# MoE with MLP and KAN experts: at least one pair of MLP blocks ahead of the first KAN layer in place of two, and ScalarE's weight copies ahead of its notes of rows

## What is computed

```python
x = x + 0.5 * moe(layernorm(x), ...)
x = x + attention_block(layernorm(x), ...)      # window of 128, 16 heads, gated FFN
x = x + 0.5 * moe(layernorm(x), ...)

# moe: 8 experts, top 2; 4 are MLPs and 4 are KANs
w_full = top-2 softmax weights of x @ gate_W     # per token
h = gelu(x @ mlp_W1 + mlp_b1)                    # 128 -> 512
mlp_out = h @ mlp_W2 + mlp_b2                    # 512 -> 128
h0 = layernorm(x, kan_ln_g0, kan_ln_b0)
basis0 = 1 - tanh((h0 - grid) / 2) ** 2          # 8 grid points: 128 -> 1024
z = basis0 @ kan_sl_W0 + kan_sl_b0               # 1024 -> 256
h1 = layernorm(z, kan_ln_g1, kan_ln_b1)
basis1 = 1 - tanh((h1 - grid) / 2) ** 2          # 256 -> 2048
kan_out = basis1 @ kan_sl_W1 + kan_sl_b1         # 2048 -> 128
out = sum of the experts' outputs by w_full
```

## Time and profile before

| | us |
|---|---|
| median of three runs | 637.17 |
| lowest and highest | 632.69, 643.67 |
| the profiled execution, whole | 639.1 |
| its span, first to last instruction | 637.3 |
| PE, DVE, ACT, POOL busy in it | 558.2, 454.3, 401.1, 262.1 |

### The profile page before, as it was taken

How to read it: one execution, slowest core, us unless ns; L and a number is a source line. 1 busy time by engine, 2 the same in 40 slices (tenths; PEclk the granted TensorE clock), 3 DMA queues, 4 the chain that set the end, 5 groups by cost and what they waited for, 6 DMA issues and landing times. The chain is left out here.

```text
span 637.3 us, 19397 instructions
## 1 busy us (share of the span) xinstructions
PE 558.2 (88%) x6514; PEld 494.5 (78%) x6515; DVE 454.3 (71%) x1135; ACT 401.1 (63%) x954; POOL 262.1 (41%) x314
## 2 busy tenths in 40 slices
PE   9677899999999488888889888998788999999970
PEld 8666899999999355766778783688788999999970
DVE  6734768788788576699678788557466787878864
ACT  4645868889875158710456523256587789888943
POOL 7144556555544345820000013221455556656540
PEclk7768989999999869999999999985798999999995
DMA  8793222100101220000100039303111000110106
GB/s 264 246 407 100 67 62 86 45 26 29 33 16 19 68 78 3 4 3 14 16 5 4 5 120 402 156 29 114 34 30 26 25 27 27 33 29 25 29 18 202
DMA packets 41433, 46.58 MB, mean 73 GB/s; under 512 B 7409, under 2 KB 33377, under 8 KB 40353
## 3 DMA queue, kind: packets, MB, share of 16 engines
q1 hardware_dynamic: 32272, 33.99, 15.9%
q0 software_dynamic: 4736, 9.71, 5.5%
q10 hardware_dynamic: 4368, 2.10, 1.1%
HBM read 35.69 MB, written 10.09 MB: 72 GB/s over the span
## 5 line engine op out<-in xcount | busy, mean ns | idle before, releaser
L881 PE MATMUL k_y_ps<-kan_w,k_basis 128*128 x1056 | 128.5, 281 | 7.3 <-DVE k_basis L978 7.3
L881 PEld LDWEIGHTS k_y_ps<-kan_w,k_basis 128*128 128x128 f32 x1056 | 124.4, 196 | 9.6 <-issue 9.2
L871 PE MATMUL k_z_ps<-kan_w,k_basis 128*128 x528 | 120.5, 381 | 0.6 <-issue 0.6
L1151 ACT ACTIVATE k_sig<-k_h1T 128x256 f32<-128x256 f32 x264 | 84.4, 402 | 47.5 <-DVE k_h1T L1005 47.4
L871 PEld LDWEIGHTS k_z_ps<-kan_w,k_basis 128*128 128x128 f32 x528 | 98.2, 191 | 13.3 <-issue 1.1
L978 DVE SCALAR_TENSOR_TENSOR k_basis<-k_sig 128x512 f32<-128x512 f32 x132 | 88.1, 690 | 14.6 <-ACT k_sig L1151 14.6
L1817 ACT ACTIVATE got<-p_ps 128x960 f32<-128x960 f32 (+1 forms) x44 | 39.2, 944 | 42.0 <-PE p_ps L1672 41.9
L1144 ACT ACTIVATE k_sig<-k_h0T 128x128 f32<-128x128 f32 x280 | 59.2, 294 | 7.6 <-DVE k_h0T L966 7.6
L697 POOL DMA_INDIRECT y_rows<-k_y,k_rows x33 | 34.3, 1041 | 53.8 <-DVE j_y L1033 28.3
L849 PE MATMUL m_z_ps<-m_xT,m_w 128*128 128x128 f32 x304 | 43.3, 289 | 8.1 <-ACT m_w L1173 4.9
L849 PEld LDWEIGHTS m_z_ps<-m_xT,m_w 128*128 128x128 f32 x304 | 41.4, 202 | 11.1 <-ACT m_w L1173 6.3
(11 more groups left out here) (270 smaller groups left out, 1089.5 us busy)
## 6 DMA issues: line engine op xcount, KB each, us to landing
kan_w<-in_L_ffn_kan_sl_W_dram SPq DMA_DIRECT2D x16, 1024.0 KB, 14.0
x_rows<-got SPq DMA_DIRECT2D x16, 256.0 KB, 2.5
mlp_w<-in_L_ffn_mlp_W_dram SPq DMA_DIRECT2D x2, 1024.0 KB, 5.9
mlp_w<-in_L_ffn_mlp_W_dram SPq DMA_DIRECT2D x8, 256.0 KB, 6.7
got<-y_rows SPq DMA_DIRECT2D x8, 256.0 KB, 4.9
got<-y_rows ACTq DMA_DIRECT2D x8, 256.0 KB, 5.4
xs<-in_L_attn_x_dram SPq DMA_DIRECT2D x4, 256.0 KB, 3.8
s_cos<-in_cos_dram SPq DMA_DIRECT2D x8, 128.0 KB
```

What stands on the lines that cost most here:

```text
L871: last = nc.tensor.matmul(z_ps, basis0[:, g], k.kan_w0[:, bass.ds(e, 1), g], start=(g == 0), stop=(g == G - 1))
L881: last = nc.tensor.matmul(y_ps, basis1[:, g, c], k.kan_w1[:, bass.ds(e, 1), c, g], start=(g == 0 and c == 0), stop=(g == G - 1 and c == F2 ...
L1151: ins = nc.scalar.activation(sig1[:, g], h1T[:], ACT.Sigmoid, bias=float(-GRID[g]))
```

## The change

It has three parts.

- DVE, L405: the lower bound under the halving goes from 5.0 to 3.0, so that `pairs` is at least 1 in place of 2. The bound asserted in `counts` follows.
- POOL: no blocks ahead of the loop any more. A pass gathers and scatters block 2 ii + 1, then block 2 ii + 2, and then waits for both stores and frees both `m_y`. The two waits behind the loop are gone.
- ACT: its loop starts at 0 as well. Only the note for block 1 stands ahead of it. In a pass the copy of the weights for block 2 ii + 4 stands ahead of the note for block 2 ii + 2, and this note waits for `m_y_free` to be 2 ii + 2, where it waited for `m_stored[1]`.

```diff
@@ route, DVE
-                link(nc.vector.tensor_scalar(pairs_i[:], spread[:], 1.0, 5.0, ALU.add, ALU.max))
+                link(nc.vector.tensor_scalar(pairs_i[:], spread[:], 1.0, 3.0, ALU.add, ALU.max))
@@ counts
-            for v, low, high in zip(found, (2, 1, 1, 9), (MAXB // 2 + 1, MAXB, MAXB, MAXB)):
+            for v, low, high in zip(found, (1, 1, 1, 9), (MAXB // 2 + 1, MAXB, MAXB, MAXB)):
@@ moe_blocks, POOL
-                for u in range(2):
-                    m_gather(1 + u, u)
-                    m_scatter(1 + u, u)
-                with pool.Fori(1, pairs) as ii:
+                with pool.Fori(0, pairs) as ii:
                     for u in range(2):
-                        j = 2 * ii + (1 + u)
-                        pool.wait_ge(m_stored[u], ii * 16)
+                        m_gather(2 * ii + (1 + u), u)
+                        m_scatter(2 * ii + (1 + u), u)
+                    for u in range(2):
+                        pool.wait_ge(m_stored[u], ii * 16 + 16)
                         pool.sem_inc(m_y_free, 1)
-                        m_gather(j, u)
-                        m_scatter(j, u)
 
                 pool.wait_ge(turned, 2)
                 pool.sem_inc(noted, 1)
                 get_rows(x_in, rows_first[:, 2], loaded)
-                pool.wait_ge(m_stored[0], pairs * 16)
-                pool.sem_inc(m_y_free, 1)
                 power(0)
                 m_scatter(2 * pairs + 1, 0)
-                pool.wait_ge(m_stored[1], pairs * 16)
-                pool.sem_inc(m_y_free, 1)
@@ moe_blocks, ACT
-                _, *e_first = mlp_experts(act, 0, 5)
+                _, *e_first = mlp_experts(act, 0, 3)
                 m_take_w1(first, e_first[0])
                 note_rows(1, 0)
-                note_rows(2, 1)
                 sigmoids0(0)
                 m_take_w1(2, e_first[1])
                 act.preload_act_table(ACT.Gelu)
                 gelu(first)
-                m_take_w1(3, e_first[2])
-                gelu(2)
-                m_take_w1(4, e_first[3])
-                gelu(3)
-                act.wait_ge(m_stored[0], 16)
-                note_rows(3, 0)
-                with act.Fori(1, pairs) as ii:
+                with act.Fori(0, pairs) as ii:
                     _, *e_pair = mlp_experts(act, 2 * ii + 2, 3)
                     m_take_w1(2 * ii + 3, e_pair[0])
                     gelu(2 * ii + 2)
-                    act.wait_ge(m_stored[1], ii * 16)
+                    m_take_w1(2 * ii + 4, e_pair[1])
+                    act.wait_ge(m_y_free, 2 * ii + 2)
                     note_rows(2 * ii + 2, 1)
-                    m_take_w1(2 * ii + 4, e_pair[1])
                     gelu(2 * ii + 3)
                     act.wait_ge(m_stored[0], ii * 16 + 16)
                     note_rows(2 * ii + 3, 0)
```

## The result

| | before | after |
|---|---|---|
| median of 11 runs each, us | 633.86 | 640.70 |
| lowest and highest | 630.4, 643.67 | 637.32, 643.9 |
| ratio of the runs, with its 95% interval | | 1.009 [1.0061, 1.0119] |
| the profiled execution, whole | 639.1 | 641.56 |
| its span, first to last instruction | 637.3 | 639.7 |

The change makes the kernel slower by 0.9%: 5.7 us, by the interval 3.9 to 7.5. The ratio compares fast runs, and two runs of before, 643.67 and 643.64, count as slow; with them the means differ by 4.2 us. The forecast was 639.8 us, which is 2.6 above the 637.2 that the three runs shown gave. The two profiled executions differ by 2.5 us. So the forecast met the difference of the profiles, and the difference of the runs is about twice that.

The account below looks back on a forecast made before the run. The prediction took TensorE (PE) to bound both mixtures. First mixture -0.4 us, second +3.0, ACT's reordering and the jumps back zero: +2.6 on the 637.2 us median of three runs, so 639.8 us, range 633 to 645.

Parts of the forecast that it names:

- A: The forecast itself, both mixtures: -0.4 us in the first, +3.0 us in the second, 639.8 us; 50%.
- D: Loops on ACT and POOL: jumps back fetch code, 1.26 us in POOL's chain on top of A, 641.1 us; 14%.
- Block counts, joint rounds: First mixture: 1 pair, 13 joint rounds of 9.25 us and 2 alone of 7.71; the second mixture keeps 2 pairs.
- First KAN matmul: First mixture: weights land at 50.4 us, then 0.5 us of register reads, so 50.9 us (50.4 to 51.7).
- First KAN group: First mixture, L871: 3.62 us at full clock plus 1.7 for one fall of the clock, 5.3 us.
- Sum of the first mixture: First KAN product 3.5 us earlier, two more joint rounds cost 3.1 us: -0.4 us (-2.6 to +0.4).
- Second mixture: POOL's new order delays PE's first KAN group by 1.3 us, plus 1.7 for the clock: +3.0 us (0.1 to 4.1).
- The bound: First mixture, one pair less ahead of KAN and two more joint rounds: -0.4 us.
- C: First mixture: the clock doesn't fall behind the wait for KAN weights either, and B holds; 634.7 us; 12%.
- E: Joint rounds: POOL's slip is carried on, 3.6 us in each of 13 rounds, 684 us, slower by over 2%; 3%.
- B: Second mixture: POOL's wait is free, x_in lands in time, the clock stays up; -0.4 + 0.1, 636.9 us; 16%.

Follow-up runs that it names:

- the order alone: The kernel before with the new order on GpSimd and ScalarE but the old bound 5.0, two pairs in both mixtures; ratio to before 0.999 [0.9949, 1.0031].
- the bound alone: The kernel before with bound 3.0 in the first mixture only, GpSimd and ScalarE in the old order; ratio to before 1.0083 [1.0049, 1.0117].
- the kernel that kept PE busy: The kernel after, with 20 repetitions of small unread matmuls ahead of PE's wait for the KAN weights; ratio to before 1.007 [1.0026, 1.0113].

## Why the prediction came out right, and where its steps were off

**The total** (640.7 against 639.8) and its place within 2% hold, and the nearness is luck. Two errors cancel in it: the median of before was 633.86 over eleven runs, 3.3 us below the 637.2 of three from which I counted, and the change was +5.7 us, 3.1 more than my +2.6. Beneath it the steps read off single profiles came mostly as written, with three sizes off. But the two parts changed places: I had the loss in the order, and the runs have it in the bound. The number doesn't tell A from D either, whose 641.1 is as near.

**Block counts, joint rounds.** 1 pair, 13 joint rounds, 2 alone; 9.25 and 7.70 us. As forecast.

**First KAN matmul, forecast 50.9, measured 53.47.** Two terms. The landing was 51.4 and not 50.4: the issue stood, its 20.8 us had become 22.0. And the 0.5 us that I took for PE's register reads behind the wait was 2.1 us; I had set 1.26 as its upper bound. I had misread the code there: a pass reads four expert numbers, but behind the wait PE reads six (two of the KAN blocks, four of the MLP blocks), so the 1.26 us of a pass bounded nothing. The term can be read without any landing in the two kernels with the narrower wait and one pair: 1.68 us of "issue" above and 1.77 in the other.

**First KAN group, forecast 5.3, measured 5.69.** One fall costs 5.69 - 3.62 = 2.1 us where I took 1.7; 5.93 in another profile, 2.3. Together the first product is 0.5 us earlier than before, by PE's ends 59.16 against 59.70, where I forecast 3.5.

**Sum of the first mixture, forecast -0.4, measured 0.0 on the first pair of profiles.** The near hit is luck. First KAN matmul -2.0; from there to the first second-layer matmul +1.3 (14.5 against 13.2, all of it the first KAN group, 5.69 against 4.42); the two joint rounds +3.1; and -2.4 because the first two rounds took 19.95 us (67.98 to 87.93) where before took 22.33 with a fall of the clock in them. That last term was in no step of mine. Over the profiles of each the length is the same to 0.2 us, though single ones of before scatter by 2 to 3.

**Second mixture, forecast +3.0 (0.1 to 4.1), measured +2.1 in length on the first pair.** POOL went as written, only later: the scatter of block 4 took 3.3 us to land where I took 2.3, and POOL took 1.0 us from that landing to its next issue (467.40 + 3.3 to 471.71), and 1.2 from the one before (460.06 + 2.3 to 463.57), where I took 0.83. The fetch of x_in came at 471.71, forecast 470.4. Counted from the first turn it is 4.4 us later than before, where I had 3.6. The pause of 3.69 us, the slow group behind it, and the first second-layer matmul 3.4 us later than before (31.7 against 28.3) are the mechanism of case A. **But as a cost of the order the +3.0 fell.** The step that failed is one I didn't see as a step: I took the single profile of before as the state of that stretch. It was the one of eight without the stall of ACT and DVE in the pairs. Against the usual execution the order costs 0.6 us in length and nothing measurable in time. For the order alone, 168.2 us in its second profile lies between the two forecasts (166.7 to 168.1, or 168.5 to 171) and settles nothing; the runs do.

**The bound, forecast -0.4, measured +5.3 us in runs by its ratio (+4.2 by the means of all runs, 642.1 against 637.9).** Here lies the other half. That the wait for the weights makes the difference is shown: with the wait narrowed the same kernel gains 1.8%, and the kernel with two pairs 0.4%. Where the microseconds pass is not. The first mixture is no longer than before in profiles. The whole profiled executions do carry a difference (644.03 and 639.35, against 639.1, 636.62 and 639.55: +3.3 in the means), but spread over the start, the stretch between the mixtures (233.9 to 238.8 us in these five, with the same code) and the second mixture, each within about what copies of one kernel differ by. In the second mixture the bound alone took 170.3 and 166.5 us; I had expected 169 to 171 for the second of them. What the low clock can take from the span at most, (1 - granted clock) x span, is 41.9 us in the mean of the timed runs of the bound alone, standard error 2.1, against 36.4, error 0.9, for before. That would be enough for the 4.2, and some of it may be falls of the clock later on. But it counts the clock of pauses too, and the kernel that kept PE busy had 36.7 and wasn't faster. This stays open.

**The rivals.** C and E are out: the clock did fall behind the wait for the weights, and no pause was carried into the joint rounds. B is out as a mechanism, for POOL's wait wasn't free; its price for the order, 0.1 us, is nearer to what the runs gave than my 3.0, as the old order pays elsewhere. **D, the jumps back.** The POOL rows leave at most 0.4 us for a jump (1.2 - 0.83), not the 1.26 of D. The Trainium skill, page "Runtime: NRT & Kernel Launch", section "Instruction fetch mechanics", has a taken branch outside the held code wait for a DMA; no pause of that kind can be told from these rows. The traces speak against it here as well: from the first turn of the second mixture to 475 us (476 in the kernel after) the queues of instructions moved three packets before and three after. The stall of ACT and DVE in the old order isn't such a fetch either, as far as the traces show: in none of the seven profiles does a packet on those queues start within the 2.8 us up to the end of the stall.

## What to carry over

Before work is taken out from ahead of a wait, see what the wait is for and when that arrives: work that lies under a landing costs little, and here most of the second pair did. The gain was in the wait itself, and came only with the wait narrowed to what the first blocks need (0.9899 against 1.0083). And a stretch that a forecast is measured against should be seen in more than one execution: here one profile in eight lacked a stall of 1.8 us, and it was the one at hand. A total that comes out doesn't prove its parts: here the bound was forecast 5.7 us too low and the order some 3 us too high.

## What the runs showed of the hardware

- **The time ahead of the first KAN group.** In the kernels with one or three pairs PE took 1.5 to 2.2 us in the first mixture from the end of the wait for the weights, or of its last matmul, to the first KAN group. With two pairs it took 0.57 us or none there, and in the second mixture 0.5 to 0.9. The same six register reads stand there in all; that they fill the time isn't shown.
- **A stall on two engines at once.** ACT and DVE, 1.7 to 2.0 us, released by "remote", in the second pass of the pairs: in 7 of 8 profiles with the old order, in none of 6 with the new. No packet of instructions starts in it. Its cause is open.
- **When the clock falls.** A pause of 2.32 us was followed by a group of 5.38 us, one of 2.43 by one of 3.62, and one of 1.86 by 5.46. The length of a pause alone doesn't tell whether the clock falls.
- **A scatter beside a load.** The scatter issued at 45.00 us, while the KAN weights were coming in, held ACT's note until 51.23; it landed after 6.1 us. The three of the second mixture, with little else moving, landed in 2.3 to 3.3 us.
- **Copies of one kernel** differ by up to 5 us in the first mixture's length. The clock accounts for it: lengths of 174.8, 176.8 and 180.0 us go with 5.5, 7.4 and 10.5 us of (1 - granted clock) x length.
